# Row maxima of half rows in the attention loop: fused sum and maximum for two of sixteen, the excess by TensorE and ScalarE

## The reference, cut to what matters

```python
attn = jnp.einsum('bhqd,bhkd->bhqk', query, key) / scale      # scale = 12
attn = jax.nn.softmax(attn, axis=-1)
out = jnp.einsum('bhqk,bhkd->bhqd', attn, value)
```

## Time and profile before

| | |
|---|---|
| median of 3 runs | 1159.34 us (1155.55 to 1163.48) |
| the profiled execution, its own time | 1156.96 us |
| its span (first to last instruction) | 1155.1 us |
| mean granted TensorE clock | 0.962 of full |
| busy: TensorE, VectorE, ScalarE, GpSimd | 1038.0, 931.4, 787.4, 318.1 us |
| attention loop | from 355 us to 950 us of the span |

### The profile page before, as it was taken

How to read it: one execution, slowest core, us unless ns; L and a number is a source line. 1 busy time by engine, 2 the same in 40 slices (tenths; PEclk the granted TensorE clock), 3 DMA queues, 4 the chain that set the end, 5 groups by cost and what they waited for, 6 DMA issues and landing times. The chain is left out here.

```text
span 1155.1 us, 23773 instructions
## 1 busy us (share of the span) xinstructions
PE 1038.0 (90%) x9049; PEld 497.4 (43%) x9049; DVE 931.4 (81%) x1461; ACT 787.4 (68%) x1536; POOL 318.1 (28%) x460
## 2 busy tenths in 40 slices
PE   6988699577778999999999999999999989999897
PEld 4776598553421222222222222222222239767655
DVE  7887454478778999999999999999999908756445
ACT  4553433144456999999999999999999984535321
POOL 4631377467530000000000000000000007055464
PEclk9999899879877999999999999999999999999999
DMA  7001366316650101111011101110010000713313
GB/s 244 1 22 53 93 193 179 121 26 181 186 190 3 30 3 30 31 30 22 11 30 32 30 3 30 30 30 18 15 30 3 2 3 7 207 36 92 90 53 94
DMA packets 60695, 71.67 MB, mean 62 GB/s; under 512 B 9892, under 2 KB 39716, under 8 KB 60072
## 3 DMA queue, kind: packets, MB, share of 16 engines
q1 hardware_dynamic: 55784, 60.30, 19.1%
q0 software_dynamic: 4800, 9.86, 3.5%
HBM read 45.02 MB, written 25.05 MB: 61 GB/s over the span
## 5 line engine op out<-in xcount | busy, mean ns | idle before, releaser
L1521 DVE TENSOR_REDUCE mx<-p_psA 128x1 f32<-128x1024 f32 x492 | 562.8, 1214 | 11.3 <-PE p_psA L1689 11.1
L1622 ACT ACTIVATE h<-p_psS 128x512 f32<-128x512 f32 x984 | 527.6, 596 | 36.0 <-PE p_psS L1745 21.1
L1776 PE MATMUL p_acc<-h,p_V 128*32 128x256 f32 x4096 | 326.3, 392 | 14.0 <-ACT attn L1600 13.3
L1745 PE MATMUL p_psS<-Q,K 51*128 51x512 bf16 x984 | 302.3, 384 | 0.4 <-DMA Q<-m_rows 0.4
L1689 PE MATMUL p_psA<-K,Q 48*128 48x512 bf16 x984 | 299.3, 386 | 2.6 <-DVE mx L1521 1.7
L1776 PEld LDWEIGHTS p_acc<-h,p_V 128*32 128x32 f32 x4096 | 82.9, 108 | 208.9 <-ACT h L1622 105.0
L1426 POOL TENSOR_TENSOR mr<-zeros,mx 128x16 f32<-128x16 f32 x32 | 7.1, 222 | 542.0 <-DVE mx L1521 532.6
L1689 PEld LDWEIGHTS p_psA<-K,Q 48*128 48x128 bf16 x984 | 54.5, 94 | 208.0 <-DVE mx L1521 159.8
L1745 PEld LDWEIGHTS p_psS<-Q,K 51*128 51x128 bf16 x984 | 59.7, 93 | 10.2 <-ACT h L1622 9.0
L1107 DVE TENSOR_TENSOR f_h<-f_bank,b 128x512 f32<-128x512 f32 x39 | 27.0, 692 | 42.1 <-PE f_bank L1175 42.1
L2157 POOL DMA_INDIRECT h<-hrows,gidx x32 | 32.1, 1003 | 48.1 <-DVE gidx L888 32.2
(11 more groups left out here) (365 smaller groups left out, 1516.7 us busy)
## 6 DMA issues: line engine op xcount, KB each, us to landing
f_w<-in_w SPq DMA_DIRECT2D x39, 256.0 KB, 3.2
Q<-q_rows SPq DMA_DIRECT2D x32, 192.0 KB, 4.7
K<-k_rows SPq DMA_DIRECT2D x32, 192.0 KB, 5.1
result<-f_shared_kept SPq DMA_DIRECT2D x11, 256.0 KB, 2.4
result<-f_y SPq DMA_DIRECT2D x9, 256.0 KB, 3.4
hrows<-h SPq DMA_DIRECT2D x4, 516.0 KB, 7.7
x<-in_x SPq DMA_DIRECT2D x4, 512.0 KB, 5.6
w<-in_w SPq DMA_DIRECT2D x1, 2048.0 KB, 9.3
```

The source lines that it names most:

```text
L1521: dve.tensor_reduce(mx[v % 2][:, h, qt:qt + 1], psA[t][:], AX.X, ALU.max).then_inc(a_max, 1)
L1622: act.activation(pt[s % 2][:, head_at(s, j), :], psS[k % 3][:], ACT.Exp, scale=INV_SCALE).then_inc(s_out, 1)
L1745: pe.matmul(psS[k % 3][:], K[g % NBUF][rows, h // 2, kc * P:(kc + 1) * P], Q[g % NBUF][rows, h // 2, half * 512:(half + 1) * 512], start=T ...
L1776: mm = pe.matmul(acc[VW * h:VW * (h + 1), cols], V[:, v0 + h * (HD + 1):v0 + h * (HD + 1) + VW], pt[s % 2][:, h, cols], start=(kc == 0 and ...
```

## The change

In steps 16, 20, 24 and so on to 252 (60 steps, two in each unit but the first two), the maximum for t = 1 is taken as in the first ten steps. `a_part` leaves out the upper half for it. A new entry of the score ring, `difference`, holds the upper half minus the lower. It is computed by two accumulating matmuls, 13 steps before its step (so in steps 3, 7, 11 and so on), in the half step t = 0 between the scores and the values. ScalarE takes its relu into SBUF (`beyond_lower`), and VectorE's `tensor_tensor_reduce` of 512 columns takes the place of the `tensor_reduce` of 1024. For each group from 1 to 15 GpSimd negates the lower half of the keys on partitions 64 to 111 (`minus`), once. The ring's numbering is now a table.

```diff
+def halved(s, t):
+    return t == 1 and 2 * KC <= s < NSTEPS and s % (KC // 2) == 0
+def difference_after(s, j):
+    return s + AHEAD + 1 if j == 1 and halved(s + AHEAD + 1, 1) else None
+def excess_of(s):
+    return s // (KC // 2) % SLOTS
...
+        minus = parts[0][0].rearrange("p a (c t) -> p a c t", c=2)
...
             # GpSimd, after the split of unit v
+                    g = v // 2 + 1
+                    if v % 2 == 0 and g < NGRP:
+                        if g == 1:
+                            for qk in range(2):
+                                pool.wait_ge(qk_stored[qk][0], 16 * STORES[qk] * (B // 2))
+                        pool.wait_ge(group_in[g % NBUF], (g // NBUF + 1) * GROUP_IN)
+                        pool.wait_ge(m_split, v + 1)
+                        upper_rows = slice(64, 64 + KROWS)
+                        pool.tensor_scalar(minus[upper_rows, g % 2, :, :], K[g % NBUF][upper_rows, :, 0:512],
+                                           -1.0, None, ALU.mult).then_inc(minus_ready, 1)
...
             # VectorE, step s
+                        if halved(s, t):
+                            over = beyond[excess_of(s)]
+                            dve.wait_ge(s_out, difference_at(s) + 1)
+                            dve.tensor_tensor_reduce(out=over, in0=psA[t][:, 0:512], in1=over, scale=1.0, scalar=-3.0e38,
+                                                     op0=ALU.add, op1=ALU.max, accum_out=mx[v % 2][:, h, qt:qt + 1]).then_inc(a_max, 1)
+                            continue
                         dve.tensor_reduce(mx[v % 2][:, h, qt:qt + 1], psA[t][:], AX.X, ALU.max).then_inc(a_max, 1)
...
             # ScalarE
+                def beyond_lower(d):
+                    k = difference_at(d)
...
+                    act.wait_ge(s_mm, k + 1)
+                    act.activation(beyond[excess_of(d)], psS[k % 3][:], ACT.Relu).then_inc(s_out, 1)
...
                         if j == 1 and s % KC == TURN and s // KC + 1 < NUNITS:
                             turned(s // KC + 1)
+                        if difference_after(s, j) is not None:
+                            beyond_lower(difference_after(s, j))
...
             # TensorE
                 def a_part(s, t, c):
+                    if halved(s, t) and c == 1:
+                        return
...
-                    if c == 1:
+                    if c == 1 or halved(s, t):
                         mm.then_inc(a_mm, 1)
+                def difference(s):
...
+                    pe.wait_ge(s_out, k - 2)
+                    if w == 0:
+                        pe.wait_ge(group_in[g % NBUF], (g // NBUF + 1) * GROUP_IN)
+                        pe.wait_ge(minus_ready, g)
+                    pe.matmul(psS[k % 3][:], Q[g % NBUF][rows, pair, q0:q0 + P], K[g % NBUF][rows, pair, 512:L], start=True, stop=False)
+                    pe.matmul(psS[k % 3][:], Q[g % NBUF][rows, pair, q0:q0 + P], minus[rows, g % 2, pair, :],
+                              start=False, stop=True).then_inc(s_mm, 1)
...
                         if t == 0 and s % KC == TURN and s // KC + 1 < NUNITS:
                             turn(s // KC + 1)
+                        if t == 0 and difference_after(s, 1) is not None:
+                            difference(difference_after(s, 1))
                         if s >= 1:
                             values(s - 1, t)
```

More of the change, by code:

```diff
@@ L1243, in declare_heads, with ring_order, difference_at @@
     M.mp = n.sb("mp", [P, P // (QUAD * 4), QUAD * 4], BF16)
+def halved(s, t):
+    return t == 1 and 2 * KC <= s < NSTEPS and s % (KC // 2) == 0
+def difference_after(s, j):
+    return s + AHEAD + 1 if j == 1 and halved(s + AHEAD + 1, 1) else None
+def ring_order():
+    order = [("turn", 0)]
+    for s in range(WIDE0):
+        for j in range(QUAD):
+            order.append(("score", s, j))
+            if j == 1 and s % KC == TURN and s // KC + 1 < NUNITS:
+                order.append(("turn", s // KC + 1))
+            if difference_after(s, j) is not None:
+                order.append(("difference", difference_after(s, j)))
+    return {entry: k for k, entry in enumerate(order)}
+SCORE_RING = ring_order()
 def score_at(s, j):
-    return 1 + s * QUAD + j + min((s * QUAD + j + (KC - TURN) * QUAD - 2) // (KC * QUAD), NUNITS - 1)
+    return SCORE_RING["score", s, j]
 def turn_at(v):
-    return 0 if v == 0 else score_at((v - 1) * KC + TURN, 1) + 1
+    return SCORE_RING["turn", v]
+def difference_at(s):
+    return SCORE_RING["difference", s]
+def excess_of(s):
+    return s // (KC // 2) % SLOTS
 def fast_before(i):
@@ L1308, in phase_project_attention1 @@
         nk = pt[0][:, 0, :].bitcast(BF16).rearrange("p (c t) -> p c t", c=2)
+        minus = parts[0][0].rearrange("p a (c t) -> p a c t", c=2)
+        beyond = [parts[0][1 + i // 2].rearrange("p c t -> p (c t)").bitcast(F32)[:, i % 2 * 512:(i % 2 + 1) * 512] for i in range(SLOTS)]
+        minus_ready = n.sem("minus_ready")
         excess = [pt[1][:, i, :] for i in range(SLOTS)]
@@ L1430, in _ @@
                     pool.tensor_tensor(mp[:, 2, :], mr[:], mp[:, 1, :], ALU.subtract).then_inc(m_split, 1)
+                    g = v // 2 + 1
[8 more added lines that the diff above has]
+                                           -1.0, None, ALU.mult).then_inc(minus_ready, 1)
+                        pool.wait_ge(minus_ready, g)
             @block.vector
@@ L1607, in above @@
                     act.activation(excess[FAST_SLOT[i]], upper[FAST_SLOT[i]], ACT.Relu).then_inc(r_ready, 1)
+                def beyond_lower(d):
+                    k = difference_at(d)
+                    if d == 2 * KC:
+                        for qk in range(2):
+                            act.wait_ge(qk_stored[qk][0], 16 * STORES[qk] * (B // 2))
+                    act.wait_ge(s_mm, k + 1)
+                    act.activation(beyond[excess_of(d)], psS[k % 3][:], ACT.Relu).then_inc(s_out, 1)
                 for i in range(2 * FAST):
@@ L1690, in a_part @@
                                    K[g % NBUF][rows, pair, c * 512:(c + 1) * 512], start=True, stop=True)
-                    if c == 1:
+                    if c == 1 or halved(s, t):
                         mm.then_inc(a_mm, 1)
+                def difference(s):
+                    g, w, k = s // GSTEPS, s % GSTEPS, difference_at(s)
+                    half, pair, qt, rows = w // KC, (w % KC) // 4, w % 4, slice(64, 64 + KROWS)
+                    q0 = (half * 4 + qt) * P
+                    pe.wait_ge(s_out, k - 2)
[5 more added lines that the diff above has]
+                              start=False, stop=True).then_inc(s_mm, 1)
                 def first_operands(s, t):
```

## The result

The changed kernel took 1191.4 us (median of 4 runs, 1187.8 to 1192.2) against 1157.4 us before on the same chip (median of 4). The ratio is 1.0264, with a 95% interval from 1.0225 to 1.0302: slower by 2.6%. The profiled execution's span is 1186.0 us against 1155.1. Forecast were 1186 us, a range from 1171 to 1199 us, and slower.

A forecast was written before the change was run, and what follows sets the result against it. TensorE's in-order work was taken to bound the loop. Its differences add 27.0 us, nothing comes off: 1156.96 + 27.0 = 1184.0 us profiled, plus 2.4 us for the median, so 1186 us, range 1171 to 1199 us.

The forecast's parts named there:

- The pace: Attention loop: TensorE's in-order work sets the 18.53 us unit, VectorE follows, so 32 us off VectorE is worth nothing.
- VectorE's reserve: Attention loop: VectorE's sixteen maxima take 18.1 us, about 0.4 us per unit short of being the bound.
- The 0.41 us gaps: TensorE's half steps: equal gaps whether VectorE's maximum or issue is named, so they are TensorE's own.
- The differences: TensorE, half step t = 0: two added matmuls cost 0.45 us for each of 60, 27.0 us in all.
- The dropped upper halves: TensorE's A part: 60 removed matmuls each ran beside a score, so nothing saved; at most 13 us.
- The ring: TensorE's waits for score entries: the new entry adds 0; upper bound 0.25 us each, 15 us.
- a stall of 0.25 us each: Rival: score entries stall at each difference as behind a turn, 42 us added, 1201 us; chance 0.12.
- The evacuation: ScalarE's copy of acc, a 1.62 us half step: it stands in other steps than the added relus; nothing taken.
- GpSimd: Fifteen key negations, 2.4 us each, at most 36 us in all, off the path and costing nothing.
- VectorE's waits: Attention loop after the change: VectorE gets new idle time, released by TensorE, some 2.4 us per unit.
- VectorE as the bound: Rival: VectorE's maxima pace the loop, so 32 us go, 1127 us at best; chance 0.06.
- the wash: Rival: A-part pairs run one after the other, so dropped halves repay half; 8 us added, 1167 us; chance 0.07.

The follow-up runs named there:

- short maxima: The kernel before, with the change's 60 maxima taken over the lower 512 columns only and nothing else changed; ratio 0.9998.
- narrow values: The kernel before, with values of the half steps t = 1 covering 16 columns instead of 256, except in a unit's first step; ratio 0.9943.
- the first two experiments: The kernel before with 60 maxima over the lower 512 columns only, ratio 0.9998; then also without the 60 upper A-part matmuls, ratio 0.9992.

## Why the prediction was right

**The pace.** Right. TensorE's order paces the loop; the short maxima, 32 us less for VectorE, changed nothing. What I had too large is VectorE's reserve. I took 16 x 1.13 = 18.1 us for its sixteen maxima and 0.4 us per unit to spare. With narrow values it needed 18.27 us, so it had 0.26 us. The 0.41 us gaps in TensorE's weight loads were its own: in the change, with VectorE waiting at several places, they are there with VectorE named (521.35) and with nothing named (522.91).

**The differences.** Right in size within 3%: 0.46 us each instead of 0.45, in the place foretold, with half steps of 1.57 us (1.55 foretold) and the others unchanged at 1.11. The reason was not the whole one. I had put the 0.45 us down to TensorE's own two matmuls. The hand-off to ScalarE and back, with a difference in it, takes 2.68 us from values to values with narrow values, and the change takes the same there, 1.11 + 1.57 us. So a cost of this size would have come by that way too. That the two agree is luck.

**The dropped upper halves.** Right: nothing, shown by their own run.

**The ring.** I took 0 and gave 0.12 to a stall of 0.25 us each. It was 0 in the change. The reason given, that the matmuls of the difference give ScalarE the time for the relu, was borne out by the run with one matmul, where the two half steps behind it grew by 0.06 and 0.04 us. What the step missed is how thin the margin is: a round of 2.14 us in a step of 2.21, and none to speak of in the step with a difference.

**The evacuation.** Not in my sum. Its half step grew by 0.03 us per unit, under 1 us in all. Among the kernels with full values it grew in every one that drops an upper A part in the half step just ahead, also in the one without differences, and in none of the others (1.62 us with all A parts kept, and where the halved steps lie at 0 and 6, at 6, or at 0 modulo 8). So it belongs to the halved A part ahead of it; I did not test why.

**GpSimd.** A negation took 2.77 us, above my upper row of 2.38. I had put the bound too low, since that row had other operands. Off the path it cost nothing, shown by its own run.

And VectorE's waits came to 57.9 us on the page, some 1.9 us per unit, where 2.4 were foretold. As the relief is worth nothing, neither moves the sum.

**The total.** 27.0 us foretold; 28.5 us by the loop's half steps (60 x 0.46 + 30 x 0.03), 30.9 us between the spans, and 2.6% (2.25 to 3.02%) in the ratio, which is 26 to 35 us. The 2.4 us between 28.5 and 30.9 are in no term of mine and stay unexplained; executions differ by as much outside the loop.

**The rivals.** VectorE as the bound and the wash both fell with the first two experiments. The caution about matmul busy time (the Trainium skill, Trainium Kernel Development and Optimization, Best Practices) spoke for VectorE, 98.5% busy; the run with short maxima, ratio 0.9998, shows that a full VectorE was no bound here. Starts told the two engines apart, busy time could not.

One statement went too far. I wrote that the difference's wait adds nothing by itself, since the values wait for the same exponential. That holds while TensorE's own work is no shorter. With narrow values the difference cost 22.0 us, though TensorE had time, because it stands between the exponential and the values.

## What to carry to other kernels

Read start to start, not busy shares: if one engine's regular piece is shorter than the other's and its pieces and stalls add up to the period, it sets the pace, however full the other looks. Here work moved to that engine cost its full time, 0.46 us for each difference, except in its one wait, where it cost 0.15 us; and relief for the engine that follows was worth nothing. The reserve of the one that follows is what it waits per unit (0.25 us here), and not what a sum of its pieces leaves (0.4 us). Before you buy relief for one limit, look for the next below it: here 32 us less for VectorE and a good part of TensorE's values taken away, both at once, made the loop only 11.9 of 571.4 us shorter, since first VectorE and then a hand-off between two engines stood close behind.

## What the runs showed of the hardware

With the difference behind the values, TensorE did not keep the order of issue between its halves. The order is difference, difference, A part, score. The first three are on partitions from 64, the score on those from 0. The score started at 525.43, ahead of the second difference (525.62) and of the A part (525.83). It is ahead of the second difference in 58 of the 59 cases that this trace holds. The Trainium skill (TensorE: Matmul & The Clock Gate, Part 2) says that matmuls stay in program order and only weight loads are pulled ahead; the measured starts differ from that, and the measurement decides. That dropping one matmul of a pair frees no time fits the same picture, in which each half works through its own list and the longer one counts; the picture itself is argued and not tested.

Of a wait of 0.5 us for ScalarE's copy, TensorE could use nearly all for two matmuls of 0.46 us. What came back, 0.14 us, came in the next two half steps, where ScalarE had the relu to do as well.
